# A four-layer graph network on one core: GpSimd waits for its row gathers behind every fourth one

## What is computed

```python
h = relu(layernorm(x))                                  # layer 0
x = x + h @ W_self.T + b_self + (segment_sum(h[src] * w, dst) / max(deg, 1)) @ W_neigh.T + b_neigh
h = relu(layernorm(x))                                  # layer 1: softmax over the edges of a node
logits = (h @ W1)[dst] - (h @ W2)[src] + d              # d: a two-layer MLP of edge_attr_3
x = x + segment_sum(softmax(logits) * ((h @ W3)[src] + d), dst)
h = relu(layernorm(x))                                  # layer 2: batch norm over all edges
m = mlp(concat(h[src], edge_attr_64)); x = x + mlp(concat(h, segment_mean(m, dst)))
h = relu(layernorm(x))                                  # layer 3
x = x + segment_sum(h[src], dst)
```

## Time and profile before

| | before |
|---|---|
| median of three timed runs | 2036.69 us (2029.17 to 2037.15) |
| span of the profiled execution | 2601.9 us |
| PE, DVE, ACT, POOL busy in it | 1601.6, 1551.6, 895.7, 1327.9 us |
| gathers of chunks (L636) | 1264, 956 ns each on average, 1208.6 us |

### The profile page before, as it was taken

The page is one execution under the profiler, slowest core; times in us unless marked ns, Lnnn a source line. Parts: engine busy times, 40 slices in busy tenths (PEclk is TensorE's granted clock), DMA queues, the critical chain, the costliest instruction groups (busy, mean ns, idle before and its releaser), DMA issues.

```text
span 2601.9 us, 23168 instructions
## 1 busy us (share of the span) xinstructions
PE 1601.6 (62%) x6953; PEld 1209.1 (46%) x6953; DVE 1551.6 (60%) x2430; ACT 895.7 (34%) x1175; POOL 1327.9 (51%) x1397
## 2 busy tenths in 40 slices
PE   1546554555565655555665247888786725889892
PEld 1334433443354444444453235666565514767672
DVE  5445545554477477677776635554555934868783
ACT  1222222222231755555553113332333811433340
POOL 6555555455534455555664455446551036656554
PEclk8566666666676777787787568898897657989896
DMA  6111211121121344444444313323224602333332
GB/s 141 36 51 54 63 52 51 53 63 52 52 68 54 99 142 145 139 141 147 145 146 129 83 37 70 69 59 75 65 65 101 204 13 53 85 78 84 78 79 57
DMA packets 223807, 219.66 MB, mean 84 GB/s; under 512 B 108066, under 2 KB 170967, under 8 KB 223447
## 3 DMA queue, kind: packets, MB, share of 16 engines
q1 hardware_dynamic: 175575, 147.75, 19.3%
q0 software_dynamic: 44384, 56.98, 10.5%
q10 hardware_dynamic: 3744, 13.63, 1.3%
HBM read 116.77 MB, written 101.46 MB: 84 GB/s over the span
## 4 chain that ended last, share of the span: by engine, by line
PE 23%; another core or an unknown queue 13%; issue 11%; DVE 11%; ACT 5%; POOL 3%; DMA 2%; SPq 1%; DVEq 0%; POOLq 0%; ACTq 0%
PE psum L993 16%; POOL arena L676 3%; PE psum L1018 1%; DVE scan_ring L1935 1%; DVE spare L1935 1%; DMA maxima<-arena 1%; DVE arena L1810 1%; PE psum L1085 1%; ACT spare L1257 1%; DVE arena L1816 1%; PE psum L1024 1%; ACT spare L1331 1%; DMA keep<-keep_rows 1%; DVE spare L1760 1%
## 5 line engine op out<-in xcount | busy, mean ns | idle before, releaser
L636 POOL DMA_INDIRECT gathered<-table,idx x1264 | 1208.6, 956 | 1014.9 <-issue 363.6
L1760 DVE COPY_PREDICATED spare<-spare,psum 64x512 f32<-64x512 uint8 x300 | 220.8, 736 | 303.7 <-ACT spare L1355 208.2
L993 PE MATMUL psum<-rounded 128*128 128x512 f32 x1144 | 303.8, 419 | 63.8 <-issue 43.4
L993 PEld LDWEIGHTS psum<-rounded 128*128 128x128 f32 x1144 | 227.3, 202 | 124.9 <-issue 59.2
L780 PE MATMUL psum<-ident,arena 128*128 128x128 f32 x416 | 107.9, 409 | 287.5 <-ACT arena L1140 272.1
L1592 DVE TENSOR_REDUCE rs<-arena 128x16 f32<-128x1024 f32 x52 | 63.4, 1219 | 302.3 <-ACT arena L1144 249.6
L780 PEld LDWEIGHTS psum<-ident,arena 128*128 128x128 f32 x416 | 69.8, 205 | 354.9 <-ACT arena L1140 284.0
L1144 ACT ACTIVATE arena<-psum 128x1024 f32<-128x1024 f32 x52 | 53.3, 1025 | 410.9 <-remote 280.3
L1355 ACT ACTIVATE spare<-psum 64x512 f32<-64x512 f32 x82 | 48.5, 592 | 397.7 <-remote 199.0
L676 POOL DMA_INDIRECT arena<-scan,rowidx x75 | 79.3, 1058 | 206.7 <-DMA scan<-ea 114.3
L906 PE MATMUL psum<-ident,arena 128*128 128x128 f32 x172 | 34.4, 335 | 189.3 <-ACT arena L1246 185.5
(11 more groups left out here) (285 smaller groups left out, 3444.9 us busy)
## 6 DMA issues: line engine op xcount, KB each, us to landing
scan<-ostage SPq DMA_DIRECT2D x130, 256.0 KB, 2.3
scan<-arena SPq DMA_DIRECT2D x52, 512.0 KB
gathered<-table,idx POOLq DMA_INDIRECT x1264
d_mlp<-arena ACTq DMA_DIRECT2D x26, 512.0 KB
arena<-d_mlp SPq DMA_DIRECT2D x52, 256.0 KB
maxima<-arena SPq DMA_DIRECT2D x52, 256.0 KB
ea<-in_edge_attr SPq DMA_DIRECT2D x104, 128.0 KB
spare<-src_row SPq DMA_DIRECT2D x100, 128.0 KB
```

The source lines that it names most:

```text
L636: pool.indirect_dma_start(out=out[:, j, hf, :], out_offset=None, in_=tab[layer], in_offset=bass.IndirectOffsetOnAxis(ap=idx[:, j, hf * NCH ...
L993: last = nc.tensor.matmul(P[:, bank + t, :], parts[layer][n][:, b:b + 2, :].rearrange("p b d -> p (b d)"), tile(layer, m, u)[:, hf * CH:(h ...
L1760: picked = v.copy_predicated(rows[m % 2][halves[hf], :], quarter[m % 2][halves[hf], q - 1, :], P[halves[q % 2], bank + q // 2, :])
```

## The change

GpSimd waits for its own gathers. `gather_chunk` gets a further argument, the semaphore's count before the chunk; in front of the fifth gather (`j == J // 2`) GpSimd waits until the first four have landed (64 more), and behind each call until all eight have (128 more). This holds for all four layers. No instruction but these waits is added, and none is moved.

```diff
-            def gather_chunk(layer, k, i, out, done):
+            def gather_chunk(layer, k, i, out, done, before):
 
                 for j in range(J):
+                    if j == J // 2:
+                        pool.wait_ge(done, before + J * 16)
                     for hf in range(2):
                         pool.indirect_dma_start(
...
-                            gather_chunk(0, k, i, Gw(k, D, m), S("gathered", 2 * m + k))
+                            gather_chunk(0, k, i, Gw(k, D, m), S("gathered", 2 * m + k), n_gathered(0, n))
+                            pool.wait_ge(S("gathered", 2 * m + k), n_gathered(0, n + 1))
...
-                    gather_chunk(1, c % 2, c // 2, Gw(g % 2, 2 * D), S("wide gathered", g % 2))
+                    gather_chunk(1, c % 2, c // 2, Gw(g % 2, 2 * D), S("wide gathered", g % 2), n_gathered(1, g // 2))
+                    pool.wait_ge(S("wide gathered", g % 2), n_gathered(1, g // 2 + 1))
...
-                gather_chunk(2, c % 2, c // 2, Gw(g % 2, D, g // 2 % 2), S("gathered", g % 4))
+                gather_chunk(2, c % 2, c // 2, Gw(g % 2, D, g // 2 % 2), S("gathered", g % 4), n_gathered(2, g // 4))
+                pool.wait_ge(S("gathered", g % 4), n_gathered(2, g // 4 + 1))
...
-                gather_chunk(3, c % 2, c // 2, Gw(g % 2, D, g // 2 % 2), S("gathered", g % 4))
+                gather_chunk(3, c % 2, c // 2, Gw(g % 2, D, g // 2 % 2), S("gathered", g % 4), n_gathered(3, g // 4, g % 4))
+                pool.wait_ge(S("gathered", g % 4), n_gathered(3, g // 4 + 1, g % 4))
```

## The result

The changed kernel takes 2583.72 us, the median of four runs (2579.21 to 2591.88), against 2036.47 us (2029.17 to 2037.15): 1.271 times as long, 95% interval 1.267 to 1.274. The forecast was 2476 us, and the result lies 9 us above the range. The direction was right; of the added time, 547 us, the prediction had 439.

The account below looks back on a forecast made before the run. GpSimd's gather issue was taken to bound the timed run. Added waits cost 156, 138, 72 and 79 us in layers 0 to 3, +445, less 6 for last waits: 2476 us from 2036.7, range 2345 to 2575.

Parts of the forecast that it names:

- the stalls: Idling around late products, in nearly every layer 0 round; GpSimd's 543.3 us of buffer waits, taken as absent from timed runs.
- The sum behind it: Whole kernel before: 1264 gathers at 1.25 us, 1580 us, plus 485 us without gathering, together 2065 us.
- The sum of the kernel before: Gathering stretches, each the larger of GpSimd's time and the others': 520, 430, 357 and 311 us, 1618 in all.
- The price of a wait: Each of 316 added waits: landing 2.5 us plus restart 0.27 less 1.25, so 1.5 us, 1.6 in layer 1.
- the cover: Part of the added waits hidden behind PE's work: 27 us in layer 2, 11 us in layer 3.
- The prediction's own upper case: All layers: landing of 2.85 us, 1.87 us a wait, 13.74 us a chunk, +552 less 7, 2582 us.
- The two anchors: Ends for a gather's landing: 2.2 us into quiet engines, 3.14 us for the slowest last-row gather of its size.
- What would show it: Signs in the profile after: gaps near 2.8 us, 316 waits of 1.5 us, layer 0 near 731 us, span under 2720 us.
- (a): Stalls and GpSimd's 543 us of idling are in the timed run too and cover the waits; some 2100 us; chance 0.06.
- (b): GpSimd issues gathers at 0.95 us in the timed run, so is not the bound before; some 2324 us; chance 0.07.
- (c): Fewer gathers in flight free the DMA engines for SP's loads and stores; faster, 1990 us; chance 0.01.
- (d): Longer gaps drop PE to its lower clock, 0.6, in layers 2 and 3; 2636 us; chance 0.04.

Follow-up runs that it names:

- the trace without stalls: Kernel before plus GpSimd waits, behind each chunk, for the chunk before it, which has long landed; chip 3: 2031.12 us timed, 2027.46 us profiled.
- a short one every four: Changed kernel, but in layers 0 and 1 each wait is for three of the last four gathers; 2559.97 us on chip 5, 2391.40 us on chip 3.

## Why the prediction was right or wrong

**What the stalls are: wrong.** "I take the stalls as the recording's own" fell. By their times they are in all runs of the kernel before on chips 7, 2 and 5, and the traces of it from chips 7 and 2 show them; on chip 3 no time and no trace has them. "No instruction of the program fills the stretch from 300.2 to 309.05" was a misreading of a full trace: GpSimd issues its gathers through it, the last of sixteen in a row at 305.19:

```profile
305.19 0.94 POOL L636 DMA_INDIRECT gathered<-table,idx  x1 [0.30 <-issue]
```

The trace of before that was shown has a span like those on the three chips, and the timed runs have the time of the fourth; that the two came from different chips is the likely reading, but no list of spans for those timed runs shows it. The conclusion drawn, that the timed run lacks the stalls, held all the same. The sum behind it, 2065 us against 2037, had two errors of opposite sign: without stalls the gathering stretches are 1623 us where it had 1580, and the rest 403 where it had 485.

**The sum of the kernel before: right as a whole.** Forecast by stretch 520, 430, 357, 311 us, measured without stalls 523, 455, 334, 310. Two errors cancel. In layer 1 GpSimd is not quite without a break (the row of gathers is 25 us longer than 43 x 10.0). In layer 2 PE does not bind: its 357 us belonged to a granted clock of 0.86, and without stalls it is 327.4 us at 0.99. The two neighbours of a stall had been read as if independent of it.

**The price of a wait: the step that failed.** The four stretches grow by 193.6, 141.4, 122.0 and 106.9 us from the trace without stalls to that of the changed kernel, 563.9 together, where the prediction had 445. (The chip of the second trace is not on record; those of the changed kernel from chips 7 and 2 have 707 and 710 us in layer 0 where it has 717.) Divided by the waits: 1.86, 1.64, 1.85 and 1.78 us, 1.78 on average. Of the prediction's two terms the cover is right as a whole, though in the wrong layers: the stretches without waits are over 10.0 us a chunk by 3, 25, 4 and 10 us, 43 together, where it had 0, 0, 27 and 11, 38 together. The price is not: the stretches after are over 10.0 us a chunk by 607 us, 1.92 us a wait, where it had 483 us, 1.5 and 1.6 a wait. The 119 us missing are these 124 less the 5 of cover.

The mis-sized term is the mean landing, 2.5 us in the prediction. As the typical landing 2.5 us is right: it is the median measured, and the middle gaps of 2.73 to 2.83 us are close to the 2.77 and 2.87 forecast. But 316 waits cost the mean. The 309 waits for gathers idle GpSimd 662.1 us, 2.14 us each, and with the 0.95 us of the gather itself the mean gap is 3.09 us; less the 0.27 us of restart, the mean landing is 2.8 us. Of the 124 us the gaps make about 91, and 17 come from the gathers of layer 0 held up beside VectorE's product, a term that the sum did not have; the remaining 16 were not traced. The prediction's own upper case, a mean landing of 2.85 us, gave 2582 us, 2 below the result; the range stopped at 2575.

The two anchors were not of one kind. The upper one, 3.14, is a row from issue to landing. The lower one, 2.2 us, is the end of a window: cut finer, the bytes of that gather stop before 277.80, 1.9 us after its start, and no gather of layer 0 lands before 2.3 us. In the quiet case the bytes stop at 1.85 us and the count comes at 2.5, and the sum had these 0.65 us nowhere. With four waits a chunk and the trace without stalls beside it, both on chip 3, layer 0 pays (862.7 - 523.0) / 208 = 1.63 us a wait; the further waits alone cost (862.7 - 709.9) / 104 = 1.47 us each by the changed kernel's stretch on chip 2, or 1.41 by the recorded 716.5. They add no gather that is held up beside VectorE: there are 39 in both kernels.

The Trainium skill, "DMA: Bandwidth & Descriptors", section "Anatomy of one DMA — SWDGE (gpsimd) path", counts the completion into its fixed cost, so its estimated 2.08 us for 32 KB stands against the landing. The trace does not agree: the median landing is 2.5 us and the shortest in layer 0 is 2.3, and the measured rows decide.

**The way from the stretches to the median.** The rest of the span is 402.7 us without waits and 403.3 with them; the 6 us credited to the last waits did not appear. The spans differ by 564.5, the medians by 547.3, because the profiled run of after is 8.2 us above its median and that of the kernel that stands for before 9.0 us below 2036.5.

**What would show it.** Gaps of 2.8 us: 2.73 to 2.83 in the middle, 3.09 on average. "316 entries, 1.5 us each": 309 entries, 662.1 us, 2.14 each, of which 0.30 are there without a wait. Waits for VectorE under 100 us: gone. Layer 0 near 731, span 2620 to 2720: 716.5 and 2590.2, as the stalls that were to stay under the waits did not stay.

**The rivals.** (a)'s premise, that timed runs have the stalls, holds on three of four chips; its consequence, 25 to 100 us slower, holds on none: the change takes the stalls away, 2577 instead of 2607 us. On the record it is out. Whether the products end late or their signal comes late is not shown. The ends are modelled; PE starts later work meanwhile (L757 at 299.85), which speaks for the signal, but it too idles 1.14 and 1.03 us before its last two L757, for no named reason, and the trace without stalls has the two back to back. (b): GpSimd's cadence of 1.25 us (1.26 on average in layer 0) holds in the run without stalls too, so it is out. (c) is out where there are no stalls; where there are, a gain came by a mechanism that it did not name. (d): PE's granted clock in layers 2 and 3 is 0.90 and 0.89 after, against 0.99 and 0.99 without pauses and stalls. It does fall, and PE is busy 28 and 23 us more, but these are the two stretches in which PE was to bind and does not: 355 us of 457 and 322 of 417.

## What to carry to other kernels

When a recorded span and a timed median differ by a fifth, first ask whether both came from one chip in one condition, and price nothing by a resource that is read beside a stall. A wait for one's own transfer costs the landing at the semaphore, not at the last byte, plus the restart, less the issue time it replaces, and it costs that in full where the waiting engine is the bound. A sum over many waits needs the mean landing, 2.8 us here, and not the typical one, 2.5. On a chip where dense gathers hold another engine up, one pause per eight gathers is worth 250 to 264 us here and two are worth 30, so a change like this is to be measured on more than one chip.

## What the runs showed of the hardware that was not expected

- Chips differ by 28% on one kernel: 2029 us on chip 3, 2607 to 2618 us on chips 7, 2 and 5. On the slower ones ScalarE starts 13 us after the modelled end (295.57) of the products that it needs, while GpSimd issues gathers without a break. A pause until the queue is empty, every four gathers, removes this in the layer that has it (no idling of ScalarE without a named releaser is left there); a pause every eight leaves 96 or 228 us of such idling in layer 0, one every sixteen 339, and a short one every four 338, of 379. With a pause every eight, at the chunk's end, all 25 idlings over 3 us end when the eighth gather lands. What in the chip does it stays open, and so does why one chip is free of it.
- 0.9 us pass from the last byte of a gather to the start of the next one that waited for it (1.85 and 2.75 us), 0.65 of them before the count, against 0.27 us from VectorE's end to such a gather.
- A gather that starts together with VectorE's product of two tiles holds GpSimd 1.39 us instead of 0.95 (39 times in layer 0 with waits, 3 times without pauses).
- With pauses PE's granted clock in layers 2 and 3 is 0.90 and 0.89, and without pauses or stalls it is 0.99 in both, at nearly the same work.
- No kernel tried beats 2029 us on the chip without stalls. On those with stalls the best is the one with middle waits alone, 2343 us, and on chip 3 it would come to an estimated 2029 + 158 x 1.78 = 2310 us; it did not run there.
